# Rows of k repeated by transfers inside SBUF for four of the eight delta steps of a chunk

## What is computed

```python
q = _l2norm((x @ Wq).reshape(b, s, nh, d))
k = _l2norm((x @ Wk).reshape(b, s, nh, d))
v = (x @ Wv).reshape(b, s, nh, d)
beta = jax.nn.sigmoid(x @ Wbeta)
def step(state, inp):
    qt, kt, vt, bt = inp
    kk = kt[..., :, None] * kt[..., None, :]
    bb = bt[..., None, None]
    state = state * (1.0 - bb * kk) + bb * (vt[..., :, None] * kt[..., None, :])
    out_t = jnp.einsum('bhij,bhj->bhi', state, qt)
    return (state, out_t)
```

## Time and profile before

| | |
|---|---|
| runs | 1813.59, 1815.94, 1822.41 us; median 1815.94 |
| the profiled execution's own time | 1819.73 us |
| its span | 1818.0 us |
| PE, PEld | 1599.6 us busy (88%), 1107.9 us (61%) |
| DVE | 1372.1 us (75%) |
| ACT, POOL | 947.3 us (52%), 917.1 us (50%) |

### The profile page before, as it was taken

The page is one execution under the profiler, slowest core; times in us unless marked ns, Lnnn a source line. Parts: engine busy times, 40 slices in busy tenths (PEclk is TensorE's granted clock), DMA queues, the critical chain, the costliest instruction groups (busy, mean ns, idle before and its releaser), DMA issues. The chain is left out here.

```text
span 1818.0 us, 34322 instructions
## 1 busy us (share of the span) xinstructions
PE 1599.6 (88%) x12535; PEld 1107.9 (61%) x12537; DVE 1372.1 (75%) x2530; ACT 947.3 (52%) x1610; POOL 917.1 (50%) x960
## 2 busy tenths in 40 slices
PE   5979998879887889888888999999999999999982
PEld 4644455446455555444444777888888778877741
DVE  5868766557766767866576798788888899898983
ACT  5622566447555656445554445566655554655510
POOL 6236747553655356477678326642221355646055
PEclk9889999889888999989899999999999999999986
DMA  8963789779878766466436756876665778877432
GB/s 270 281 168 101 197 236 291 225 211 264 246 232 244 231 161 156 135 157 166 143 105 181 226 200 202 258 218 195 192 197 189 221 220 265 248 232 224 136 98 79
DMA packets 284392, 363.69 MB, mean 200 GB/s; under 512 B 32688, under 2 KB 213040, under 8 KB 278080
## 3 DMA queue, kind: packets, MB, share of 16 engines
q1 hardware_dynamic: 243168, 297.68, 56.8%
q0 software_dynamic: 17056, 33.66, 6.5%
q10 hardware_dynamic: 24000, 30.15, 4.8%
HBM read 207.51 MB, written 121.90 MB: 181 GB/s over the span
## 5 line engine op out<-in xcount | busy, mean ns | idle before, releaser
L1469 POOL DMA_INDIRECT xs_dram<-sc_in,pos x256 | 267.7, 1046 | 144.5 <-issue 66.6
L1443 POOL DMA_INDIRECT gat<-ys_dram,pos x256 | 271.8, 1062 | 120.7 <-issue 62.8
L2063 DVE TENSOR_REDUCE row_max<-R 128x6 f32<-128x768 f32 x256 | 239.8, 954 | 112.1 <-PE R L1015 55.5
L934 PE MATMUL R<-ident_b 128*128 128x512 bf16 x1001 | 281.1, 403 | 21.3 <-issue 4.0
L1480 POOL TENSOR_SCALAR_AFFINE_SELECT probs<-probs 128x512 f32<-128x512 f32 x256 | 175.3, 685 | 224.6 <-ACT probs L1641 219.7
L1641 ACT ACTIVATE probs<-R 128x768 f32<-128x768 f32 x256 | 203.6, 808 | 120.9 <-PE R L1039 95.0
L1158 PEld LDWEIGHTS Y<-fd,hid 128*128 128x128 f32 (+1 forms) x1680 | 221.2, 192 | 47.1 <-DVE hid L2213 18.7
L1158 PE MATMUL Y<-fd,hid 128*128 128x128 f32 (+1 forms) x1680 | 239.0, 280 | 10.3 <-DVE hid L2213 10.1
L1489 POOL TENSOR_TENSOR o_acc<-o_acc,read 128x512 f32<-128x512 f32 x98 | 128.0, 1306 | 215.0 <-DVE read L2170 213.6
L901 PE MATMUL R<-fhl,fw 128*128 128x512 f32 (+1 forms) x484 | 190.6, 394 | 1.6 <-issue 1.0
L934 PEld LDWEIGHTS R<-ident_b 128*128 128x128 bf16 x1001 | 93.0, 101 | 146.6 <-issue 55.0
(11 more groups left out here) (282 smaller groups left out, 3463.2 us busy)
## 6 DMA issues: line engine op xcount, KB each, us to landing
fw<-wf SPq DMA_DIRECT2D x44, 1408.0 KB
q_rows<-kq SPq DMA_DIRECT2D x128, 256.0 KB, 5.3
fx<-xs_dram SPq DMA_DIRECT2D x74, 256.0 KB
fd<-in_L_ffn_w_dram SPq DMA_DIRECT2D x44, 320.0 KB
xs_dram<-gat SPq DMA_DIRECT2D x24, 512.0 KB, 5.2
qk_dram<-qk_parts SPq DMA_DIRECT2D x32, 384.0 KB
Q<-qk_dram SPq DMA_DIRECT2D x64, 192.0 KB
K<-qk_dram SPq DMA_DIRECT2D x64, 192.0 KB
```

Of the source, the lines that this page charges most:

```text
L934: pe.matmul(psum["R"][:, b * C:(b + 1) * C], ident_b[:, :], ident_b[:, :].unsqueeze(1).to_broadcast([P, TILES, P]), start=True, stop=True)
L1443: pool.indirect_dma_start(gat[:, i % 2, 2 * t + a, :], None, ys_dram[l][g], bass.IndirectOffsetOnAxis(ap=pos[l][g][a][:, col:col + 1], axi ...
L1469: pool.indirect_dma_start(xs_dram[g], bass.IndirectOffsetOnAxis(ap=pos[l][g][a][:, col:col + 1], axis=0), sc_in[:, n % 2, t * P:(t + 1) * ...
L2063: dve.tensor_reduce(row_max[:, b, :, :, h2].rearrange("p c g -> p g c"), pair[:, :].rearrange("p (g c t) -> p g c t", g=2, t=P)[:, :, 0:3, :],
```

## The change

For the columns j = 2, 3, 6 and 7 the product is dropped. In its place step LK issues four more transfers of 256 KB a chunk, of the same form as those of q, from the rows of k in `kq` to two new tiles `k_rows` (one for each half of the chunk, laid over tiles that routing no longer needs); a half is now six transfers and not four, all counted on one semaphore, of which there are six in turn and not four. DVE reads the row from `k_rows` and not from PSUM. ACT waits for DVE by a new semaphore. The steps that waited for the last product of a chunk wait for that of j = 5. The planner is told the new lengths (LK 4.8 and not 3.6), that D2 of those columns needs LK and no bank, a `LANDED` of 11.0, and some of its due times are set anew, so that it writes another order.

```diff
+ROWS_BY_DMA = (2, 3, 6, 7)
+PICKED = [j for j in range(HD) if j not in ROWS_BY_DMA]
...
-    APART, LANDED = ("SC", "CG", "EG"), 9.0
+    APART, LANDED = ("SC", "CG", "EG"), 11.0
...
-        return tb + (21.13 * j if j < fast else 20.9 * fast + 21.50 * (j - fast))
+        return tb + (21.13 * j if j < fast else 20.9 * fast + 22.49 * (j - fast))
...
-                stage(t + 6 + k, "LK", n, k, after=[("D1a", n, 0, "DVE")] + since(n, 1, ("DS", 4 * k + 3, "DVE")), SP=3.6)
-            stage(t + 6, "D1b", n, after=[("D1a", n, 0, "DVE")], ACT=(whole, since(n, 1, ("D2", HD - 1, "PE"))), DVE=odd)
+                stage(t + 6 + k, "LK", n, k, after=[("D1a", n, 0, "DVE")] + since(n, 1, ("DS", 4 * k + 3, "DVE")), SP=4.8)
+            stage(t + 6, "D1b", n, after=[("D1a", n, 0, "DVE")], ACT=(whole, since(n, 1, ("D2", PICKED[-1], "PE"))), DVE=odd)
...
+                free = [("DS", n, j - 2, "DVE")] if j >= 2 else since(n, 1, ("DS", HD - 2 + j, "DVE"))
+                if j in ROWS_BY_DMA:
+                    stage(s, "D2", n, j, after=[(("LK", n, j // 4, "SP"), later)] + free, DVE=1.22, ACT=0.54)
+                else:
+                    stage(s, "D2", n, j, after=[("D1b", n, 0, "DVE")], PE=0.54, DVE=(1.22, free), ACT=0.54)
+                    banks("D2", n, j, ("D2", n, j, "DVE"))
...
-        decay_made, read_made, rows_loaded = signal("decay_made", HD), signal("read_made", HD), slots("rows_loaded", 4)
+        decay_made, read_made, rows_loaded = signal("decay_made", HD), signal("read_made", HD), slots("rows_loaded", 6)
+        dw_made = signal("dw_made", len(ROWS_BY_DMA))
...
                         sp.dma_start(q_rows[:, j, :], kq[j::HD, 1, :].unsqueeze(1).to_broadcast([H, HD, C]))\
                           .then_inc(rows_loaded.sem(2 * n + k), 16)
+                        if j in ROWS_BY_DMA:
+                            sp.dma_start(k_rows[k][:, j % 2, :], kq[j::HD, 0, :].unsqueeze(1).to_broadcast([H, HD, C]))\
+                              .then_inc(rows_loaded.sem(2 * n + k), 16)
...
-                    wait(*kb.filled())
-                    dve.tensor_tensor(dw[:, k % 2, :, :], kb[:, :].unsqueeze(1).to_broadcast([P, 2, C]), nb[:, :, :],
-                                      ALU.mult).then_inc(kb.free, 1)
+                    if k in ROWS_BY_DMA:
+                        wait(*rows_loaded(2 * n + k // 4))
+                        row, done = k_rows[k // 4][:, k % 2, :], dw_made.sem
+                    else:
+                        kb = bank_of["kb", n, k]
+                        wait(*kb.filled())
+                        row, done = kb[:, :], kb.free
+                    dve.tensor_tensor(dw[:, k % 2, :, :], row.unsqueeze(1).to_broadcast([P, 2, C]), nb[:, :, :],
+                                      ALU.mult).then_inc(done, 1)
```

More of the change, by code:

```diff
@@ L339, in hw @@
     def hw(j):
-        return tb + (21.13 * j if j < fast else 20.9 * fast + 21.50 * (j - fast))
+        return tb + (21.13 * j if j < fast else 20.9 * fast + 22.49 * (j - fast))
     f0_start = a_time(7) + 121.14
-    f0 = [f0_start + 8.80 * f - 95.63 * (f >= NT[0][0]) for f in range(sum(NT[0]))]
+    f0 = [f0_start + 8.80 * f - 87.99 * (f >= NT[0][0]) for f in range(sum(NT[0]))]
     def experts0():
@@ L430, in table @@
         g = group(0, n)
-        c.append(max(hw(2 * n + 3.6) + 32.10, f0[sum(NT[0][:g + 1]) - 1] + 12.00, (c[-1] if c else 0) + 12.74))
+        c.append(max(hw(2 * n + 3.6) + 24.65, f0[sum(NT[0][:g + 1]) - 1] + 12.00, (c[-1] if c else 0) + 12.74))
     c_end = [c[n] + 31 for n in LAST[1]]
@@ L807, in two_layer_kernel @@
         q_rows = sb("q_rows", [P, HD, C])
+        k_rows = [nc.alloc_sbuf_tensor_at(f"k_rows{half}", [P, 2, C], F32, offset=at)
+                  for half, at in enumerate((early_rows, late_rows))]
         assert top_f[0] <= 229344 - HD * C * 4
@@ L1113, in _ @@
                     project(("gate", n), 1, W1_G, halves(xd[:, :, :]))
-                if kind == "D2" and k < HD:
+                if kind == "D2":
                     if k == 0:
@@ L1726, in _ @@
                         act.activation(th[:, :], bank[:, :], ACT.Tanh, scale=0.5).then_inc(gate_tanh.sem, 1)
-                if kind == "D2" and k < HD:
-                    wait(*bank_of["kb", n, k].released())
+                if kind == "D2":
+                    if k in ROWS_BY_DMA:
+                        wait(*dw_made(n, ROWS_BY_DMA.index(k) + 1))
+                    else:
+                        wait(*bank_of["kb", n, k].released())
                     d = dw[:, k % 2, 0, :].rearrange("p (b s) -> p b s", s=S)[:, :, 1:S]
```

24 lines of the change are left out of this document (12 added, 12 removed).

## The result

The changed kernel takes 1860.07 us (median of 4 runs, 1859.23 to 1862.71). The kernel before, run beside it, takes 1819.18 (1813.59 to 1826.4). The ratio is 1.0226, 95% interval [1.0189, 1.0264]: slower by 2.3%, some 41 us. I had predicted 1800, range 1780 to 1822, and 0.16 for slower.

The account below looks back on a forecast made before the run. PE was taken to set the pace, 96% busy in the stage, DVE with slack. -28.8 + 3.5 + 4 + 0 + 1 + 5 = -15.3 us gave 1804.4 profiled, 1800 as median; range 1780 to 1822.

Parts of the forecast that it names:

- Term 4: SP's issues of the added transfers: queue held 5.0 us longer a chunk, covered in a normal chunk, price 0.
- term 5: POOL's waits for the rows: each half complete some 5 us later, hidden by idle time; +1 us, between -5 and +8.
- Term 3: DVE's `dw` reading two SBUF tiles waits for POOL's additions: 8.0 us on DVE, half taken, +4 us (0 to 19).
- rival B: DVE takes over as the bound in the stage, every `dw` waiting long: 1815.6 us, no change; chance 0.13.
- Term 1: 55 dropped products leave PE's list in the stage at 0.52 us each, all on the path: -28.8 us.
- Term 2: 16 more fillers on PE in the stage at 0.22 us each: +3.5 us.
- Term 6: The end after the last down product: more fillers ahead of the `o_acc` transposes, +5 us, ends 0 and +10.
- C: The rows land late for DVE's reads, 2.5 us a chunk in 13 chunks: 1833 us, slower; chance 0.13.
- A: The saving comes whole or more: dearer products, stalls only changing places, end hidden by DVE; 1786.6 us; chance 0.14.

Follow-up runs that it names:

- e4: The changed kernel without POOL's waits for the rows ahead of twelve indirect transfers; 1.0173 of the kernel before.
- e1: The changed kernel without the four added transfers a chunk, `dw` reading the rows of q in SBUF instead; 1.0005 of the kernel before.
- e15: The kernel before with `dw` of columns 2, 3, 6, 7 reading a row from SBUF, products still made, run a second time; 1.0137 of the kernel before.
- e2: The kernel before with `dw` of columns 2, 3, 6, 7 reading a row from SBUF, products still made, same order; 1.0169 of the kernel before.
- e10: The kernel before, same order, products of columns 2, 3, 6, 7 cut to one matmul of 64 columns, row still from PSUM; 0.9994 of the kernel before.
- e13: The kernel before, same order, with both the products cut to one of 64 columns and the row read from SBUF; 1.0104 of the kernel before.
- e14: The changed kernel without the four added transfers a chunk, run a second time; 1.0010 of the kernel before.
- e11: The changed kernel with LK's second half a later step of its own and 6.0 us told to the planner for each half; 1.0194 of the kernel before.
- e6: The changed kernel with the added transfers issued from POOL's queue, those of chunk 0 staying with SP; 1.0185 of the kernel before.
- e3: The kernel before with the added transfers into tiles that nobody reads, nothing else changed; 1.0237 of the kernel before.
- e9: The kernel before with the added transfers, read by nobody, at 256 columns and not 512, half the bytes; 1.0077 of the kernel before.

## Why the prediction was wrong

**Term 4, transfers and SP, price 0: the step that failed.** The added transfers measured +2.2 to 2.6%, about +40 us, POOL's waits of term 5 included; without those, e4 against e1, it is 33 us, and that alone gives the sign. I took the hold at 5 us a chunk from the earlier trace rows (it is 7) and closed with "no wait of PE for them is among the stage's, and three buffers are ahead". Both halves of that were beside the point. That PE does not wait for a load today says nothing of its slack; in the trace of before the least time from a landed load to its first use is 0.9 us. And three buffers are no cover by themselves: a load is issued only when the block three before it is done and takes 10.8 us, which in the trace of before leaves 0.9 to 21 us until its first use, 8.8 in the median, against lags of up to 9.4 us now. I could have read the lag and the slack of the 44 loads from the trace of before; I checked cover only for the readers of the rows.

**The clock: not in the sum at all.** The earlier trace rows show 1.00 in full stretches, and I took that as given. With the waits for weights it falls: 58 us of the stage at the lower level, 10.5 before. Six of the ten stretches at the lower level, 41 of the 58 us, begin within such a wait or less than 1 us behind it, the other four behind waits of 1.2 to 1.9 us for DVE or ACT. It is about half of the transfers' cost in the stage (18.8 of 34.0 us).

**Term 3, DVE's two tiles of SBUF, +4: mechanism right, size wrong.** The flat PSUM form, the waits for additions and the tail came as written. But the mean in the stage is 1467 ns in the changed kernel, 0.25 us over its median, and up to 1539 in the others (e15), where I had 0.145 from the scans; and "I take half" was wrong, in e2 and e15 nearly all of it is on the path. Measured alone it is 14 to 16 us of the stage, 1.4 to 1.7% of the time, near my upper end of 19. The rule of the Trainium skill ("SBUF — State Buffer", "Who interferes with whom"), that the two exclude each other for a whole instruction, is what the timelines show in both directions (1.98 and 2.20 us). It was the warning that deserved the weight of rival B.

**Term 1, products, -28.8, "I take it all as the path's": wrong.** PE does lose 13 to 15 us in e10 and e13 by the cut, and the time loses nothing while the order stays. A share of 96% with 14 to 19 us of waits for `hid` in it is two engines taking turns, not one bound. As work the term was well sized: from e15 to e14 PE's busy time falls by 22.7 us, where terms 1 and 2 have 25.3. With the order planned anew the stage gives back 20.5 us, which pays for term 3 and little more: terms 1 to 3 sum to -21.3 us in the prediction and to 0.05 and 0.10% in e1 and e14, with intervals from -0.2 to +0.4%. Term 2, the fillers, no run measures alone.

**Term 5, POOL's waits, +1.** Between 0.5 and 0.9%, beyond my upper end of +8 us. The rows' later landing is passed on to gathers and scatters; some 5 us of it are in the end.

**Term 6, the end, +5.** It is 89.1 us and not 88.2, but the size is luck on both sides. The 88.2 of the profile that I read is 4 to 6 us longer than the end of the same list in six other runs; against those the change adds 5 to 7 us, and by POOL, not by fillers: with POOL's waits gone (e4) or the transfers (e1, e14) it is 83.6 to 83.9 us with all 206 fillers in it.

**The rivals.** C had the right sign by the wrong place. DVE waited 0.8 us for rows, where I had 13 chunks of 2.5; the lateness went to the transfers issued *behind* the rows. B's mechanism is real and brought the change to no gain before the transfers' cost came on top, but not by its own sign: DVE is busy 91% of the stage in e1 (639.7 of 704 us) and PE 95%. A is out.

**What stays open.** How the 41 us divide between late loads, the clock and the time ahead of the stage exactly, since no run here holds the clock and the last varies from run to run. Why e11 and e6, with less than half of the waits for weights, are only 0.3 to 0.8% faster than the change; they have other orders and other waits. And whether some order makes the dropped products pay on top of the port: none was found that beats the kernel before. In the old order (e3), how much the late loads and how much POOL's waits for the rows cost.

## What to carry to other kernels

Price a transfer by what stands behind its issue in the same in-order queue: for each load there take the time from free buffer to first use, less its flight, and see if the issues put ahead fit in; that nobody waits for the load now is no answer. Ask too which other engine waits for the last of the transfers. Before counting work taken from the busiest engine as time, see whom it still waits for: where two engines take turns, the saving may come only with a list planned anew, and a longer instruction on the other engine is paid in full. Where an operand moves from PSUM to SBUF on DVE, count the other engine's instructions that it will now meet, in both directions.

## What the runs showed of the hardware

- An issue on an in-order queue isn't free of the bytes: of the twelve 256 KB issues of a chunk in the changed kernel the first three take 0.6 to 0.75 us (medians), those behind them 1.05 to 1.4 and up to 2.7, half the bytes in four of them shorten the row from 15.7 to 13.8 us (e9), and on ACT's queue they hold ACT's own instructions, 4.76 us for two.
- PE's clock can fall behind a short wait: after one of 1.88 us, ending at 1247.36, the windows view shows 0.57 for 1248 to 1252, and after the one of 5.97 us it shows 0.50. It does not always: one of 1.72 us, ending at 1592.3, was followed by no lower level.
- A `dw` can be held by an addition that starts after it. In the changed kernel one starts at 1197.94, within an indirect transfer, the addition starts 0.57 us later and runs its normal length, and `dw` ends 1.10 us behind it, as in four of e2 (timelines of DVE and POOL). 17 others that started during an indirect transfer were not held. What tells the two apart is open.

```profile
1197.94 2.95 DVE L2175 TENSOR_TENSOR dw<-k_rows,nb 128x1024 f32<-128x1024 f32 x1
...
1197.53 0.96 POOL L1482 DMA_INDIRECT xs_dram<-sc_in,pos  x1 [0.30 <-issue]
1198.51 1.28 POOL L1502 TENSOR_TENSOR o_acc<-o_acc,read 128x512 f32<-128x512 f32 x1
```
